# Second attention of a gated transformer block: the normalised delta moves from VectorE to ScalarE and GpSimd

## The reference

```
x = x + tanh(g_xattn[0]) * xattn0(layernorm(x), ctx)      # 8 x 128 tokens, 256 features
x = x + tanh(g_ffn[0])   * bitnet_ffn(layernorm(x))
x = x + tanh(g_xattn[1]) * xattn1(layernorm(x), ctx)      # the second attention
x = x + tanh(g_ffn[1])   * gated_ffn(layernorm(x))        # the second feed-forward

def xattn1(h, a):                    # 16 heads of 16 features
    q, k, v = h @ Wq.T + bq, a @ Wk.T + bk, a @ Wv.T + bv
    p = softmax(masked(clip(q k / 4, -50, 50)))
    delta = clip(residual_scale, 0, 0.3) * ((p v) @ Wo.T + bo)
    return (delta - mean) / sqrt(var + 1e-5) * gamma + beta
def gated_ffn(h):
    return (silu(h @ w_gate.T) * (h @ w_up.T)) @ w_down.T   # hidden size 1024
```

## Time and profile before

| | |
|---|---|
| median of 3 runs | 263.72 us (263.62 to 264.2) |
| the profiled execution | 264.11 us, of which 262.3 us is its span |
| PE, PEld busy | 212.0 us (81%), 174.5 us (67%) |
| DVE busy | 181.0 us (69%) |
| ACT busy | 132.8 us (51%) |
| POOL busy | 83.9 us (32%) |

### The profile page before, as it was taken

One profiled execution on the slowest core, in us unless ns is written; L12 is line 12 of the kernel. 1 busy time (PEld: TensorE's weight loads), 2 busy tenths in 40 slices (PEclk: granted clock), 3 DMA queues, 4 the chain that ended last, 5 costly groups with the idle time before them and its releaser, 6 DMA issues.

```text
span 262.3 us, 4538 instructions
## 1 busy us (share of the span) xinstructions
PE 212.0 (81%) x1658; PEld 174.5 (67%) x1658; DVE 181.0 (69%) x457; ACT 132.8 (51%) x296; POOL 83.9 (32%) x108
## 2 busy tenths in 40 slices
PE   0285557979889889897798688775999999999992
PEld 0264325858778778786576466654877888888882
DVE  2769879598988988786428999998984333262333
ACT  1138874478667667679755455553322323222220
POOL 2301111175856856868505333442100000000000
PEclk9999955699999999999959999997999999999999
DMA  5999003900000000000000000000000000020002
GB/s 169 369 390 301 5 0 139 343 1 0 2 0 0 2 1 0 2 2 0 0 2 2 0 2 4 0 4 0 2 2 0 0 0 2 0 80 2 0 0 80
DMA packets 9238, 12.55 MB, mean 48 GB/s; under 512 B 1025, under 2 KB 7937, under 8 KB 9217
## 3 DMA queue, kind: packets, MB, share of 16 engines
q1 hardware_dynamic: 8784, 12.07, 13.3%
q10 hardware_dynamic: 432, 0.20, 0.4%
HBM read 11.22 MB, written 1.05 MB: 47 GB/s over the span
## 4 chain that ended last, share of the span: by engine, by line
PE 50%; DVE 27%; ACT 7%; DMA 6%; issue 4%; POOL 3%; SPq 1%; DVEq 0%; ACTq 0%; POOLq 0%
PE PB L1259 16%; PE PB L1278 7%; DMA WRAW<-w_dram 6%; PE PB L1073 6%; PE PB L1172 4%; PE PB L1085 3%; DVE XV L524 3%; PE PB L1108 2%; PE PB L1112 2%; DVE HBQ L742 2%; PE PB L1019 2%; DVE RD L728 2%; DVE HBQ L572 2%; ACT SIL L906 2%; DVE HSD L578 2%
## 5 line engine op out<-in xcount | busy, mean ns | idle before, releaser
L1259 PE MATMUL PB<-SGN,WHI 128*128 128x512 f32 x128 | 40.5, 397 | 0.0
L1073 PE MATMUL PB<-SGN,XQH 128*128 128x512 f32 x64 | 27.7, 433 | 1.3 <-DVE XQL L553 1.3
L699 DVE TENSOR_TENSOR WRAW<-WRAW,PB 128x512 f32<-128x512 f32 x16 | 11.0, 686 | 24.0 <-ACT WRAW L993 23.9
L1278 PE MATMUL PB<-WHI,SGN 128*128 128x256 f32 x128 | 25.6, 283 | 2.2 <-DVE SGN L707 1.8
L1073 PE MATMUL PB<-SGN,XQL 128*128 128x512 f32 x64 | 27.1, 424 | 0.0
L289 POOL TENSOR_TENSOR RSTD<-MVS,MHALF 128x1 f32<-128x1 f32 x24 | 13.4, 560 | 40.9 <-DVE MVS L401 40.9
L1259 PEld LDWEIGHTS PB<-SGN,WHI 128*128 128x128 f32 x128 | 22.9, 188 | 4.5 <-issue 0.2
L1259 PE MATMUL PB<-SGN,WLO 128*128 128x512 f32 x64 | 25.2, 394 | 0.0
L993 ACT ACTIVATE WRAW<-PB 128x512 f32<-128x512 f32 x16 | 9.6, 600 | 28.0 <-PE PB L1259 28.0
L1278 PEld LDWEIGHTS PB<-WHI,SGN 128*128 128x128 f32 x128 | 20.7, 188 | 3.6 <-DVE SGN L707 2.4
L316 POOL TENSOR_TENSOR HBQ<-HBQ,HR 128x512 f32<-128x512 f32 x16 | 17.6, 1098 | 17.2 <-DVE HR L590 17.2
(11 more groups left out here) (122 smaller groups left out, 545.7 us busy)
## 6 DMA issues: line engine op xcount, KB each, us to landing
WRAW<-w_dram SPq DMA_DIRECT2D x2, 2048.0 KB, 12.1
X<-x_dram SPq DMA_DIRECT2D x2, 512.0 KB, 5.8
CTXT<-ctxt_dram SPq DMA_DIRECT2D x1, 1024.0 KB, 9.6
CTX<-ctx_dram SPq DMA_DIRECT2D x1, 1024.0 KB, 12.0
WRAW<-w_dram SPq DMA_DIRECT2D x1, 1024.0 KB, 14.9
WQK<-wqkvo_dram SPq DMA_DIRECT2D x1, 1024.0 KB, 7.8
WRAW<-wd_dram SPq DMA_DIRECT2D x1, 1024.0 KB, 10.1
out_dram<-X SPq DMA_DIRECT2D x4, 256.0 KB, 2.2
```

What stands on the lines that cost most here:

```text
L1073: mm = nc.tensor.matmul(PB[2 * half + m][:], part[:, p, c, :], sgn(m, c, a, b), start=(c == 0 and k == 0), stop=(c == DC - 1 and k == 1))
L1259: mm = nc.tensor.matmul(PB[2 * b + m][:], wcol(w_part, m, c, j), act_part[:, c, g * TG:(g + 1) * TG], start=(c == 0 and i == 0), stop=(c = ...
L1278: mm = nc.tensor.matmul(down_bank(g, k), act_part[:, b, ts], wdown(w_part, j), start=(j == 0 and i == 0 and k % 2 == 0), stop=(j == FC - 1 ...
```

## The change

DVE no longer forms D2 and X. It writes the negated mean (NM2) beside VE2. POOL forms RSTD2 and the offset OFF2 = NM2 * RSTD2, ACT forms D1 = DL * RSTD2 + OFF2 with a scale and an offset for each partition (`centred`), and POOL forms D2 = D1 * GAM and X = X + D2. With this everything behind it comes one step later: the statistics of X at step t are those of tile t - 2, and `norm_d`, `hi_d`, `lo_d` and the transpose `xd_t` take tile t - 3. The transpose of XD goes into the second half of PB 6 instead of PB 7, so it also waits until OT has read the first half. On ACT the exponentials of a tile are taken one step earlier. In step 8 and in the first feed-forward blocks the orders of PE, DVE and ACT differ, since three tiles are now left for them instead of two.

```diff
@@ GpSimd, step_c
                 if live(t - 2):
-                    rstd(t - 2, t - 2 + 2 * NT)
+                    pool.wait_ge(c_ve, t - 1)
+                    nc.gpsimd.tensor_tensor(RSTD2[:], VE2[:], MHALF[:], ALU.pow
+                                            ).then_inc(c_r2, 1)
+                    pool.wait_ge(c_r2, t - 1)
+                    nc.gpsimd.tensor_tensor(OFF2[:], NM2[:], RSTD2[:], ALU.mult
+                                            ).then_inc(c_of, 1)
+                if live(t - 3):
+                    rstd(t - 3, t - 3 + 2 * NT)
                 if live(t + 1):
                     v_tile(t + 1, 1 - p)
+                if live(t - 2):
+                    pool.wait_ge(c_d1, t - 1)
+                    nc.gpsimd.tensor_tensor(D2[:], D1[:], GAM[:], ALU.mult).then_inc(c_d2, 1)
+                    pool.wait_ge(c_d2, t - 1)
+                    pool.wait_ge(c_xb, t - 1)
+                    nc.gpsimd.tensor_tensor(X[:, t - 2, :], X[:, t - 2, :], D2[:], ALU.add
+                                            ).then_inc(x_done, 1)
...
-                if live(t - 1):
-                    pool.wait_ge(c_ve, t)
-                    nc.gpsimd.tensor_tensor(RSTD2[:], VE2[:], MHALF[:], ALU.pow
-                                            ).then_inc(c_r2, 1)
@@ VectorE, step_c
+                if t == NT:
+                    gu_d(0)
                 if live(t - 1):
                     dve.wait_ge(c_dn, t)
                     nc.vector.reciprocal(RD[:], PB[7][:, 0:D]).then_inc(c_rd, 1)
                 if live(t + 2):
                     norm(t + 2, p, 2)
+                if live(t - 3):
+                    norm_d(t - 3)
+                if t == NT:
+                    lo_gu(0)
...
-                if live(t - 1):
-                    nc.vector.scalar_tensor_tensor(
-                        out=D2[:], in0=DL[:], scalar=MV2[:, 0:1], in1=GAM[:],
-                        op0=ALU.subtract, op1=ALU.mult).then_inc(c_d2, 1)
-                if live(t - 1):
-                    dve.wait_ge(c_d2, t)
-                    dve.wait_ge(c_r2, t)
-                    dve.wait_ge(c_xb, t)
-                    nc.vector.scalar_tensor_tensor(
-                        out=X[:, t - 1, :], in0=D2[:], scalar=RSTD2[:], in1=X[:, t - 1, :],
-                        op0=ALU.mult, op1=ALU.add).then_inc(x_done, 1)
-                    stats(t - 1, 1 - p, t - 1 + 2 * NT)
@@ ScalarE
+            def centred(u):
+                act.wait_ge(c_of, u + 1)
+                need(act, c_d2, u)
+                nc.scalar.activation(D1[:], DL[:], ACT.Identity, bias=OFF2[:], scale=RSTD2[:]
+                                     ).then_inc(c_d1, 1)
             warm(ACT.Exp)
             copy_ht(1, 1, 4, xt_done, c_q, c_ht, 2 * NT)
+            for b in range(4):
+                exp_c(0, 0, b)
             pipeline(step_c, lag=0)
@@ TensorE
+            def xd_t(u):
+                pe.wait_ge(d_ln, u + 1)
+                pe.wait_ge(c_o, min(u + 3, NT))
+                need(pe, d_hl, u)
+                for c in range(DC):
+                    mm = nc.tensor.transpose(PB[6][:, D + c * P:D + (c + 1) * P],
+                                             XD[:, c * P:(c + 1) * P], ident[:])
+                mm.then_inc(d_t, 1)
...
             for n in range(NG * FC):
-                if n == 2:
-                    step_c(NT + 1, 1)
                 down_d(n)
+                if n in (1, 3):
+                    xd_t(NT - 2 + n // 2)
```

More of the change, by code:

```diff
@@ L128, in gated_block @@
         MV2 = sb("MV2", [P, 2])
+        NM2 = sb("NM2", [P, 1])
         VE2 = sb("VE2", [P, 1])
         RSTD2 = sb("RSTD2", [P, 1])
+        OFF2 = sb("OFF2", [P, 1])
         XH = sb("XH", [P, 2, D])
@@ L743, in step_c @@
                                             EXP_LO, ALU.min, ALU.max).then_inc(c_p, 1)
+                if live(t - 3):
+                    lo_d(t - 3)
                 if t == NT:
-                    gu_d(0)
-                    lo_gu(0)
+                    stats(t - 2, p, t - 2 + 2 * NT)
+                    gu_d(1)
                 if live(t - 1):
                     dve.wait_ge(c_dl, t)
+                    need(dve, c_d1, t - 1)
                     nc.vector.scalar_tensor_tensor(
@@ L786, in update_d @@
                         in1=X[:, t, :], op0=ALU.mult, op1=ALU.add).then_inc(x_done, 1)
-            gu_d(1)
-            lo_gu(1)
-            norm_d(NT - 1)
             for n in range(2, NG * FC):
                 gu_d(n)
+                if n in (2, 4):
+                    norm_d(NT - 3 + n // 2)
+                if n in (3, 5):
+                    lo_d(NT - 3 + n // 2)
                 lo_gu(n)
                 if n == 2:
-                    lo_d(NT - 1)
+                    stats(NT - 1, 1, 3 * NT - 1)
                 if n >= FC and n % FC == 1:
@@ L999, in _ @@
             warm(ACT.Silu)
-            silu_d(0)
-            hi_gu(0)
-            hi_d(NT - 2)
-            silu_d(1)
-            hi_gu(1)
-            for n in range(2, NG * FC):
+            for n in range(NG * FC):
+                if n in (3, 5):
+                    hi_d(NT - 3 + n // 2)
                 silu_d(n)
+                if n == 0:
+                    centred(NT - 2)
                 hi_gu(n)
-                if n == 2:
-                    hi_d(NT - 1)
+                if n == 0:
+                    hi_d(NT - 3)
+                if n == 1:
+                    centred(NT - 1)
         @block.tensor
@@ L1176, in heads, with head_sums, head_values, delta @@
                 return mm
+            def head_sums(u, p):
+                pe.wait_ge(c_p, u + 1)
+                need(pe, c_rd, u)
+                heads(7, lambda h: ONE2[:, h % 2, :], p).then_inc(c_dn, 1)
+            def head_values(u, p):
+                pe.wait_ge(c_v, 2 * u + 2)
+                need(pe, c_o, u)
+                need(pe, d_hl, u - 2)
+                heads(6, lambda h: V1[:, p, h, :], p).then_inc(c_pv, 1)
+            def delta(u):
+                pe.wait_ge(c_o, u + 1)
+                need(pe, c_de, u)
+                for c in range(DC):
+                    mm = nc.tensor.matmul(PB[5][:, 0:D], OT[:, c * P:(c + 1) * P],
+                                          WQK[:, 3, c, :], start=(c == 0), stop=(c == DC - 1))
+                mm.then_inc(c_dl, 1)
+            def xd_t(u):
+                pe.wait_ge(d_ln, u + 1)
+                pe.wait_ge(c_o, min(u + 3, NT))
+                need(pe, d_hl, u)
+                for c in range(DC):
+                    mm = nc.tensor.transpose(PB[6][:, D + c * P:D + (c + 1) * P],
+                                             XD[:, c * P:(c + 1) * P], ident[:])
+                mm.then_inc(d_t, 1)
             def scores(t, p):
@@ L1215, in step_c @@
                     xt_c(t + 2, p)
+                if live(t - 3):
+                    xd_t(t - 3)
                 if t == NT:
```

83 lines of the change are left out of this document (36 added, 47 removed).

## The result

The changed kernel takes 262.87 us (median of 20 runs, 261.38 to 265.72) against 264.29 for before (20 runs, 263.33 to 266.42): a ratio of 0.9938 with an interval of 0.9916 to 0.9961. The ratio leaves out five slow executions of the changed kernel (265.36 to 265.72, more than 1.5% above its fastest); with them the means give 0.9966. Measured again beside three of the experiments it was 0.9978 (0.9956 to 1.0001; 12 runs, median 263.12). So it is a little faster, by 0.2 to 0.6%, and the interval of the second measurement just reaches no change. 264.9 and "slower" had been forecast; the time lies inside the range of 261.5 to 267.0.

The account below looks back on a forecast made before the run. DVE was taken to bound the kernel from about 126 to 195 us, then PE. Terms -3.9 + 0.6 - 1.2 + 0.9 + 1.7 + 1.0 + 2.1 = +1.2 gave 265.3 profiled, so 264.9 us predicted, range 261.5 to 267.0.

Parts of the forecast that it names:

- Stretch 1: Start to DVE's reciprocal of tile 2: -3.9 us, bounds -2.5 to -4.6.
- the one for the two steps: Within stretch 1: the two steps after the start save 2.5 us, as work leaves DVE or goes into a later step.
- the one for the exponentials: Within stretch 1: with all four exponentials ahead of `q_out`, `q` starts 1.4 us earlier.
- the waiting for POOL: Within stretch 1: DVE waits about 0.9 us for POOL in the two steps that follow the start.
- Stretch 2: Three full steps, tile 2 to tile 5, at 7.4 instead of 7.20 us each: +0.6, bounds -0.3 to +1.5.
- the case that was put at 1.5: In a middle step POOL's D2 starts before DVE's norm, and the clamp comes 1.5 us late.
- Stretch 3: Reciprocal of tile 5 to that of tile 6: 6.6 instead of 7.78 us, -1.2.
- Stretches 4, 5 and 7: Tile 6 to gate_up_d(0), +0.9; gate_up_d(0) to gate_up_d(2), +1.7; TensorE's clock falling behind longer idle stretches, +2.1.
- the 2.1 taken for the clock: Clock falls behind two longer PE idle stretches: 1.3 for the first, 0.8 for the second; bounds 0 and 3.4.
- The price of 1.7 for the fall in before: Before, the granted clock at 0.50 for 3.4 us (179.60 to 183.00) was taken to cost half of it, 1.7.
- Stretch 6: Transposes in the feed-forward loop wait 0.5 and work 0.2, twice; with smaller gaps +1.0, bounds +0.3 to +1.4.
- the offload pays: Rival: DVE and POOL overlap freely or POOL's additions fall elsewhere, steps take 6.2, time about 260.0; chance 0.13.
- The clock holds: Rival: the two idle stretches bring no fall, or slow time lies on spare heads; 262.8 to 264.0; chance 0.25.

Follow-up runs that it names:

- the run with the exponentials put back: The changed kernel with ScalarE's exponentials back in the old order (those of tile t in step t): 266.9 us, 1.0116 of before.
- the one with the exponentials alone: The kernel before with only ScalarE's exponentials in the new order, D2 and X staying on DVE: 261.95 us, 0.9919 of before.
- the run with both repairs: The changed kernel with gate_up_d(1) ahead of `xd_t` in step 8 and POOL's D2, X and beta behind the clamp: 257.11 us, 0.9755 of before.
- the one with the earlier block: The run with both repairs, with gate_up_d(0) moved from step 8 into PE's idle stretch of step 7: 255.43 us, 0.9678 of before.
- the best version: Both repairs and the earlier block, plus seven unread matmuls on PE ahead of `q` of tile 2: 254.21 us, 0.9617 of before.
- the filler: Seven matmuls whose result nobody reads, ahead of `q` of tile 2 on PE; added to the changed kernel: 0.997 of before.

## Why the prediction was wrong

**Stretch 1 is the step that failed**: -3.9 with bounds of -2.5 to -4.6, where -6.08 and -4.77 were measured, although the earlier stages ended 0.65 and 0.37 later than in before (first scores at 125.45 and 125.17, against 124.80). It is the one stretch outside its bounds in both profiles. Of its two terms the one for the two steps was too small, the one for the exponentials was a little too large, and a third, the clock at the start, was put at nothing without a reason. Behind it stands the reading that DVE limits the whole attention: in the earlier trace rows DVE is at 4 and 2 tenths in the two slices from 124.6 to 137.8, so the start had another limit. The reciprocal of tile 0 in before (that of tile 2 is in the earlier trace rows), then both in the first profile, with an XH between them, and both in the second:

```profile
136.73 1.76 DVE L728 RECIPROCAL RD<-PB 128x256 f32<-128x256 f32 x1 [4.84 <-PE PB L1172]
...
134.64 1.76 DVE L744 RECIPROCAL RD<-PB 128x256 f32<-128x256 f32 x1 [3.99 <-PE PB L1198]
141.86 0.32 DVE L431 TENSOR_SCALAR XH<-X,MVS,RSTD 128x256 f32<-128x256 f32 x1
145.82 1.75 DVE L744 RECIPROCAL RD<-PB 128x256 f32<-128x256 f32 x1
...
135.91 1.76 DVE L744 RECIPROCAL RD<-PB 128x256 f32<-128x256 f32 x1 [5.53 <-PE PB L1198]
147.13 1.75 DVE L744 RECIPROCAL RD<-PB 128x256 f32<-128x256 f32 x1
```

The two steps after the start were to give 2.5. From the reciprocal of tile 0 to that of tile 2 it was 15.17 before, 11.18 and 11.22 after: 4.0. Most of this is the offload's: 11.99 in the run with the exponentials put back, 14.60 in the one with the exponentials alone. The prediction counted instructions and overlooked that DVE was idle in these steps, as the timeline of before shows in brackets:

```profile
140.87 0.48 DVE L749 SCALAR_TENSOR_TENSOR DL<-PB,RES,BO 128x256 f32<-128x256 f32 x1 [0.62 <-PE PB L1222]
...
143.11 0.48 DVE L769 SCALAR_TENSOR_TENSOR X<-D,RSTD,X 128x256 f32<-128x256 f32 x1 [0.50 <-DVE D L762]
```

Both waits of before are gone after the change (1.12 less, against a new one of 0.56 for the heads). XH in the second of these steps takes 0.32, not 0.72 (0.40 less). And the waiting for POOL, put at 0.9, was 0.28: only the two clamps were longer, 1.42 instead of 1.28. 2.5 + 0.56 + 0.40 + 0.62 is 4.1.

The early exponentials were put at 1.4, by which `q` would start earlier; it starts 0.96 earlier, less than that. But the first reciprocal comes 2.74 and 1.19 earlier, counted from the first scores. What goes beyond 0.96 is the clock, which the prediction took at the seam only: 1.78 in the first profile, 0.23 in the second. In before `q` took 2.08 and the heads of tile 0 took 1.94 twice; PE in the first profile after, where the clock was 1.00 from 130 to 175:

```profile
132.41 1.16 PE L1186 MATMUL PB<-HT,WQK 128*128 128x128 f32 x8 [1.05 <-ACT HT L836]
133.50 1.08 PE L1198 MATMUL PB<-HBQ,ONE 128*32 128x128 f32 x32
```

That the early order makes a fall at the start less likely isn't shown: the run with both repairs and the one with the earlier block have the early order too, and each was at 0.50 for about 6.6 us there.

**Stretch 2** had the right mechanism and a price too high: 7.19 where 7.4 was taken, at the lower end of 7.1 to 7.7, since the clamp ended 4.88 behind the reciprocal instead of 3.91, so 0.97 late where 0.95 to 1.5 had been summed. OFF2 took 0.19 where 0.4 was taken, so D2 did start ahead of XH, the case that was put at 1.5; it cost less because the clamp did not wait for beta. POOL's D2 took 0.72, as the sum had it, against DVE's 0.48: half as long again, not twice. **Stretch 3** was right (-1.2; -1.16 and -1.14). **Stretches 4, 5 and 7**, the seam with its clock, were to cost 4.7 and cost 6.55 and 3.84; the idle stretch ahead of the transpose was 2.46 (2.65 forecast). Behind the idle stretch of 3.36 the clock fell in one profile and not in the other, behind that of 2.46 in both. The longer blocks and Wo came to about 4.3 us in the first profile and 1.6 in the second; the 2.1 taken for the clock lies between them. The price of 1.7 for the fall in before was too high: it lies across the end of stretch 3, and the run with the exponentials alone, which had no such fall, was 0.7 shorter in stretches 3 and 4 together. **Stretch 6**: waits of 0.31 and 0.33 where 0.5 was taken, +0.7 instead of +1.0.

For the median what counts is the second profile: stretch 1 gave 0.9 more, stretch 2 cost 0.5 less, the seam 0.9 less, stretch 6 0.3 less; with rounding that is the 2.5 from +1.2 to -1.30. Stretch 1 alone would have left +0.3, so for the median the sign turned only with the other three.

Of the rivals, "the offload pays" needed D2 to start behind the clamp's beginning. It doesn't in this change; where an experiment put it there, the step was 6.41 (6.2 forecast) and the time 260.32 (260.0 forecast). "The clock holds" gave 262.8 to 264.0, where the time lies, but its reason is not what happened: falls at the seam came in both profiles. That the time lies there, and inside the wide range, owes more to luck than to that reason.

## What to carry to other kernels

Work moved from VectorE to GpSimd is worth what the two engines' instructions beside each other leave of it: here 1.03 us less of VectorE per step gave 0.01, and one wait that moved three GpSimd additions behind the clamp gave 0.78. When one more step of delay is put into a pipeline, look at the transition to the next stage: a transpose ahead of ready matmuls cost 1.2 to 1.6% (0.9817 against 0.9938 and 0.9978), and changing places took it back. And when summing steps at the start of a stage, count idle time and granted clock there as well, not only the instructions.

## What the runs showed of the hardware

At its idle stretches TensorE's clock falls in some executions and not in others: after 3.36 us of waiting ahead of the same transpose it fell to 0.50 for 6.8 us in one profile of the changed kernel and stayed at 1.00 in the other, and after 2.32 us ahead of the heads of tile 6 it fell in before and stayed at 1.00 in the run with the exponentials alone. The twenty runs of the changed kernel spread over 4.3 us with it: its three runs at a mean granted clock of 0.961 took 261.4 to 261.7, its four at 0.929 took 265.45 to 265.72. The six runs of the best version, which was at 1.00 from 128 to 196 in its profile, spread over 1.0 us; without the filler six runs spread over 3.2. In the changed kernel with the filler the clock fell at 150.5, when PE had waited for 0.80 and for 0.79 us with a transpose between them; the same two waits (0.79 each) brought no fall in either profile without the filler. A GpSimd product of one column took 0.19 us, where the power took 0.55.
